# Softmax denominators by accumulating transfers in a fused cross-attention kernel on Trainium2

## The reference

```python
xq  = (1 + scale_q)  * norm(x_q)  + bias_q      # scale and bias from silu(t_vec) @ Wss + bss
xkv = (1 + scale_kv) * norm(x_kv) + bias_kv
q = (xq @ Wq + bq)                              # 4096 x 16 x 32
k, v = split(xkv @ Wkv + bkv)                   # 3202 x 16 x 32 each
attn = softmax(q k^T / sqrt(32))                # per head, over 3202 keys
out = x_q + ((attn @ v) @ Wp + bp)
```

## Time and profile before

| | |
|---|---|
| median of 3 runs | 2140.96 us (2140.28 to 2142.82) |
| profiled execution | 2138.16 us |
| its span, first to last instruction | 2136.4 us |
| granted tensor clock | 0.999 of full speed |
| busy: PE, DVE, ACT, POOL | 2114.3, 1923.6, 1802.1, 17.3 us |
| transfers | 212.35 MB, 35.1% of the 16 engines' span on SP's queue |

### The profile page before, as it was taken

How to read it: one execution, slowest core, us unless ns; L and a number is a source line. 1 busy time by engine, 2 the same in 40 slices (tenths; PEclk the granted TensorE clock), 3 DMA queues, 4 the chain that set the end, 5 groups by cost and what they waited for, 6 DMA issues and landing times.

```text
span 2136.4 us, 56258 instructions
## 1 busy us (share of the span) xinstructions
PE 2114.3 (99%) x25036; PEld 604.5 (28%) x25036; DVE 1923.6 (90%) x1197; ACT 1802.1 (84%) x1923; POOL 17.3 (1%) x28
## 2 busy tenths in 40 slices
PE   7999999999999999999999999999999999999998
PEld 3444322222222222222222222222222222222222
DVE  2435799999999999999999999999999999999998
ACT  1212799999999999999999999999999999999995
POOL 0001000000000000000000000000000000000000
PEclk9999999999999999999999999999999999999999
DMA  9346534223422343223422342223432332232321
GB/s 314 115 161 235 148 86 97 77 80 92 118 75 77 95 102 86 67 80 92 121 71 82 89 122 71 78 79 89 110 83 71 101 95 78 70 84 78 97 55 52
DMA packets 202260, 212.35 MB, mean 99 GB/s; under 512 B 18838, under 2 KB 136222, under 8 KB 202012
## 3 DMA queue, kind: packets, MB, share of 16 engines
q1 hardware_dynamic: 199468, 208.16, 35.1%
q10 hardware_dynamic: 2544, 0.53, 0.1%
HBM read 170.38 MB, written 38.26 MB: 98 GB/s over the span
## 4 chain that ended last, share of the span: by engine, by line
PE 98%; DVE 1%; DMA 0%; issue 0%; ACT 0%; POOL 0%; SPq 0%; DVEq 0%
PE bank L1152 40%; PE bank L1164 37%; PE bank L1222 5%; PE bank L1184 5%; PE bank L1056 4%; PE bank L1067 4%; PE bank L1195 1%; PE bank L1280 1%; PE bank L1036 0%; DVE stats L1507 0%; PE bank L1207 0%; DMA arena<-in_L_xcond_Wss_kv_dram 0%; DVE arena L1525 0%; PE bank L1001 0%; PE bank L1097 0%
## 5 line engine op out<-in xcount | busy, mean ns | idle before, releaser
L1411 ACT ACTIVATE arena<-bank,shift 128x1024 f32<-128x1024 f32 x1600 | 1692.5, 1114 | 132.9 <-PE bank L1152 131.4
L1738 DVE TENSOR_TENSOR arena<-arena 128x2048 f32<-128x2048 f32 x736 | 1641.3, 2283 | 60.7 <-ACT arena L1411 59.0
L1152 PE MATMUL bank<-qs,ks 32*64 32x512 f32 x12800 | 918.2, 613 | 1.2 <-ACT arena L1369 0.7
L1164 PE MATMUL bank<-arena,vg 128*32 128x512 f32 x6400 | 852.3, 605 | 1.2 <-ACT arena L1411 1.2
L1164 PEld LDWEIGHTS bank<-arena,vg 128*32 128x32 f32 x6400 | 125.9, 108 | 650.5 <-ACT arena L1411 650.5
L1152 PEld LDWEIGHTS bank<-qs,ks 32*64 32x64 f32 x12800 | 205.0, 129 | 366.4 <-ACT arena L1411 227.0
L1222 PE MATMUL bank<-wp,arena 128*32 128x168 f32 (+2 forms) x2464 | 153.6, 321 | 0.0
L1184 PE MATMUL bank<-xt,wq 128*32 128x256 f32 (+2 forms) x2016 | 143.0, 355 | 0.0
L1222 PEld LDWEIGHTS bank<-wp,arena 128*32 128x32 f32 x2464 | 80.1, 110 | 184.3 <-issue 165.4
L1369 ACT ACTIVATE arena<-bank,bk_c 128x512 f32<-128x512 f32 (+1 forms) x28 | 17.9, 642 | 128.6 <-PE bank L1056 120.5
L1184 PEld LDWEIGHTS bank<-xt,wq 128*32 128x32 f32 x2016 | 65.5, 110 | 150.8 <-issue 132.8
(11 more groups left out here) (97 smaller groups left out, 384.9 us busy)
## 6 DMA issues: line engine op xcount, KB each, us to landing
ks<-k_full SPq DMA_DIRECT2D x160, 320.0 KB, 3.1
vg<-v_full SPq DMA_DIRECT2D x160, 320.0 KB, 3.8
p_b<-p_tails SPq DMA_DIRECT2D x128, 128.0 KB, 4.2
arena<-in_x_dram SPq DMA_DIRECT2D x15, 1024.0 KB, 9.8
q_full<-qs SPq DMA_DIRECT2D x32, 256.0 KB, 2.0
out_dram<-arena SPq DMA_DIRECT2D x32, 256.0 KB, 2.5
x_normal<-arena SPq DMA_DIRECT2D x7, 1024.0 KB, 7.6
xin<-x_normal SPq DMA_DIRECT2D x28, 256.0 KB, 10.1
```

Source lines behind the costliest of these rows:

```text
L1152: mm = nc.tensor.matmul(bank[out, 2 * (i % RING) + h % 2, :], ks[rows_of(h), keys], qs[rows_of(h), g, :], start=True, stop=True)
L1164: mm = nc.tensor.matmul(bank[rows_of(h), o_bank(u), :], vg[:, t, rows_of(h)], pt[t % PR][:, h, :], start=(t == 0), stop=False, skip_group_ ...
L1411: nc.scalar.activation(pt[t % PR][:, 2 * pair:2 * pair + 2, :], bank[:, first:first + 2, :], ACT.Exp, scale=SCALE, bias=shift[:, g:g + 1]) ...
L1738: nc.vector.tensor_tensor(a[:, :, :], (pt[t - 1] if k <= 2 else a)[:, :, :], pt[t % PR][:, :, :], ALU.add).then_inc(p_added, 1)
```

## The change

The tensor engine no longer forms the sums over keys, except for the last unit. Instead:
- `first_folds` (SP) copies partitions 0 to 31 of `acc` and `odd`, for each of the four heads, into a tile `folds` of 2 x 512 per partition, 32 partitions a head.
- `fold` (POOL) adds partitions 32 to 63, 64 to 95 and 96 to 127 onto it with three rounds of four accumulating transfers, and a fourth round adds the tail keys' weights. Each round waits for the one before, head by head.
- VectorE joins the two halves and finishes the sum over 32 partitions with its 32 x 32 transpose and a reduction, inverts, spreads the reciprocal by a second transpose, and multiplies (`sum_folds`, `invert`, `spread`, `divide` in steps 11 to 14 of the next unit), for each unit rather than for each block. `l_sums` and `l_recip` in DRAM are no longer used for this.
- The 24th add is made for the last unit alone.
- The residual is made in DRAM for blocks 0 to 6: SP copies 512 rows of x to the output (`copy_x`), POOL adds the bias (`add_bias`) and each row tile (`add_output`) with accumulating transfers. Block 7 keeps the former way.
- Query projections are cut in three parts (176, 168, 168) in all units. Output and query projections now start right after one another: steps 1 to 12 and 13 to 23 for g > 0, with two pieces in step 23; for g = 0, 1 to 12, tail scores in 13, output projection in 16 to 23 as before.
- `on` has two buffers, by the block's parity; the last buffers `l_blk`, `l_t`, `l_a`, `l_c`, `r_blk`, `r_few` go.

The diff, cut to its core:

```diff
             def q_parts(m):
-                return 3 if m == NG - 1 else 2
+                return 3
...
             def added(u):
-                return ADDS * u
+                return (ADDS - 1) * u
+            FOLDS = P // DH
...
+                    def first_folds(u):
+                        sp.wait_ge(p_added, added(u + 1))
+                        if u == 0:
+                            sp.wait_ge(xs_out[4], 16)
+                        else:
+                            sp.wait_ge(l_step, 5 * (u - 1) + 2)
+                        for h in range(HG):
+                            sp.dma_start(folds[rows_of(h), :, :], both[u % 2][0:DH, :, h, :]).then_inc(fold_in, 16)
...
+                    def copy_x(b):
+                        sp.dma_start(out2[b * QB:(b + 1) * QB, :], x2[b * QB:(b + 1) * QB, :]).then_inc(x_copied[b % 2], 16)
...
                             if u > 0:
                                 load_kv(u, NC - 1)
+                                first_folds(u - 1)
                             if more:
                                 load_kv(u + 1, 0)
-                            if g == 1 and b > 0:
-                                store_y(b - 1, 0)
-                            if u > 0:
-                                store_l(u - 1)
...
-                                store_r(b - 1, NH)
-                                load_r(b - 1, NH)
                                 store_q(b, 3)
...
-                            if g > 0 and b > 0:
-                                store_y(b - 1, g)
...
+                    def add_bias(b):
+                        pool.wait_ge(x_copied[b % 2], 16 * (b // 2 + 1))
+                        pool.dma_start(out2[b * QB:(b + 1) * QB, :],
+                                       bp.rearrange("(a n) -> a n", a=1).broadcast_to([QB, H]),
+                                       accum_op=ALU.add).then_inc(b_added[b % 2], 16)
+                    def add_output(b, j):
+                        if j == 0:
+                            pool.wait_ge(b_added[b % 2], 16 * (b // 2 + 1))
+                        pool.wait_ge(job_taken, JOB[y_last(b, j)] + 1)
+                        pool.dma_start(out2[b * QB + j * P:b * QB + (j + 1) * P, :], y_sb[:, j, :],
+                                       accum_op=ALU.add).then_inc(y_out[j], 16)
+                    def fold(u):
+                        b, g = divmod(u, NG)
+                        for s in range(1, FOLDS + 1):
+                            for h in range(HG):
+                                if s == 1:
+                                    pool.wait_ge(fold_in, 16 * HG * (u + 1))
+                                else:
+                                    pool.wait_ge(folded[h], 16 * (FOLDS * u + s - 1))
+                                if s < FOLDS:
+                                    pool.dma_start(folds[rows_of(h), :, :], both[u % 2][s * DH:(s + 1) * DH, :, h, :],
+                                                   accum_op=ALU.add).then_inc(folded[h], 16)
+                                else:
+                                    if h == 0:
+                                        pool.wait_ge(pt_out, 16 * NG * (b + 1))
+                                    row = (g * HG + h) * TAIL
+                                    pool.dma_start(folds[h * DH:h * DH + 1, :, :],
+                                                   pt_dram[row:row + TAIL, b * QB:(b + 1) * QB].unsqueeze(0),
+                                                   accum_op=ALU.add).then_inc(folded[h], 16)
+                    for u in range(1, UNITS):
+                        b, g = divmod(u, NG)
+                        fold(u - 1)
+                        if b > 0 and g == 0:
+                            add_bias(b - 1)
+                        if b > 0:
+                            add_output(b - 1, g)
...
                     def first_side(u, b, t):
-                        if b > 0:
-                            if 1 <= t < 5:
-                                project_queries(u, b, 3, 0, t - 1)
-                            if 5 <= t < 7:
-                                denominators(u, u - 1, t - 5)
...
+                        if b > 0 and 1 <= t < 13:
+                            project_queries(u, b, 3, (t - 1) // FT, (t - 1) % FT)
+                        if t == 13:
                             tail_scores(u, b)
+                        if b > 0 and 16 <= t < 24:
+                            output(u, b - 1, 0, (t - 16) // NG, (t - 16) % NG)
                     def later_side(u, b, g, t):
...
+                        if b > 0 and 1 <= t < 13:
+                            output(u, b - 1, g, (t - 1) // NG, (t - 1) % NG)
+                        if b + 1 < NB and 13 <= t < 24:
+                            project_queries(u, b + 1, g - 1, (t - 13) // FT, (t - 13) % FT)
+                        if b + 1 < NB and t == 23:
+                            project_queries(u, b + 1, g - 1, 2, FT - 1)
...
+                    def sum_folds(v):
+                        for h in range(HG):
+                            dve.wait_ge(folded[h], 16 * FOLDS * (v + 1))
+                        nc.vector.tensor_tensor(folds[:, 0, :], folds[:, 0, :], folds[:, 1, :], ALU.add).then_inc(l_step, 1)
+                        dve.wait_ge(l_step, 5 * v + 1)
+                        nc.vector.transpose(blocks(l_sb[:, :]), blocks(folds[:, 0, :])).then_inc(l_step, 1)
+                    def invert(v):
+                        some = slice(v * QB // DH, (v + 1) * QB // DH)
+                        dve.wait_ge(l_step, 5 * v + 2)
+                        nc.vector.tensor_reduce(l_keep[:, some], blocks(l_sb[:, :]), op=ALU.add, axis=AX_X).then_inc(l_step, 1)
+                        dve.wait_ge(l_step, 5 * v + 3)
+                        nc.vector.reciprocal(r_keep[:, some], l_keep[:, some]).then_inc(l_step, 1)
+                    def spread(v):
+                        some = slice(v * QB // DH, (v + 1) * QB // DH)
+                        dve.wait_ge(l_step, 5 * v + 4)
+                        nc.vector.transpose(blocks(r_sb[:, :]), r_keep[:, some].unsqueeze(2).broadcast_to([P, QB // DH, DH])
+                                            ).then_inc(l_step, 1)
+                    def divide(v):
+                        b, g = divmod(v, NG)
+                        dve.wait_ge(l_step, 5 * v + 5)
+                        dve.wait_ge(tail_added, TAIL * (v + 1))
...
+                        nc.vector.tensor_tensor(on[b % 2][:, g, :], o_all[:, g, :], r_sb[:, :], ALU.mult).then_inc(on_ready, 1)
...
+                    def vector_side(u, t):
+                        b, g = divmod(u, NG)
+                        if u > 0:
+                            if t == 11:
+                                sum_folds(u - 1)
+                            if t == 12:
+                                invert(u - 1)
+                            if t == 13:
+                                spread(u - 1)
+                            if t == 14:
+                                divide(u - 1)
+                        if g == 0 and b + 1 < NB and t == 18:
                             turn_queries(b + 1)
...
                             if k == 1 and u >= 2:
-                                dve.wait_ge(job_done, DONE["l", u - 2] + 1)
...
+                                for h in range(HG):
+                                    dve.wait_ge(folded[h], 16 * FOLDS * (u - 1))
```

More of the change, by code:

```diff
@@ L220, in attention @@
             y_out = [sem(f"y_out{j}") for j in range(TPB)]
+            last_out = [sem(f"last_out{j}") for j in range(TPB)]
             turned = sem("turned")
@@ L1188, in project_queries @@
                             mm.then_inc(job_done, 1)
-                    def denominators(u, of, half):
-                        if half == 0:
-                            free(("l", of))
-                            pe.wait_ge(p_added, added(of + 1))
-                        for h in range(HG):
-                            mm = nc.tensor.matmul(bank[rows_of(h), side_bank(u), halves_of(half)], ones[:, :],
-                                                  acc[of % 2][:, h, halves_of(half)], start=True, stop=True,
-                                                  skip_group_check=True)
-                        if half == 1:
-                            mm.then_inc(job_done, 1)
                     def tail_scores(u, b):
@@ L1676, in add_bias, with range_so_far @@
+                    def range_so_far():
+                        some = slice(0, (UNITS - 1) * QB // DH)
+                        nc.vector.reduce_max(l_tops[:, 0, 0:1], l_keep[:, some], AX_X).then_inc(last_step, 1)
+                        nc.vector.reduce_max(l_tops[:, 1, 0:1], r_keep[:, some], AX_X).then_inc(last_step, 1)
+                    def add_bias():
+                        dve.wait_ge(xy_in, 16)
                         dve.wait_ge(bp_in, 16)
-                        rows = xy[b % 2]
@@ L1678, in add_bias @@
```

(8 more changed lines are left out.)

276 lines of the change are left out of this document (76 added, 200 removed).

## The result

| | before | changed |
|---|---|---|
| median of 9 runs | 2140.92 us | 2147.93 us |
| lowest to highest | 2139.08 to 2142.82 | 2143.92 to 2157.91 |
| profiled execution, its span | 2138.16, 2136.4 | 2157.91, 2156.1 |

The ratio is 1.0037, 95% interval 1.0023 to 1.0052: slower, by 7 us on the medians, where 20 us less had been forecast. The nine runs of the changed kernel lie 14.0 us apart, those of the kernel before 3.7. Its profiled execution is the slowest of the nine, 10 us above the median, so that the trace shows the trouble larger than the median has it.

A forecast was written before the change was run, and what follows sets the result against it. PE's steps were taken as the bound, other engines covered. Gains 13.4 + 2.4 + 2.7 + 1.8 = 20.3 us gave 2120.7 on the median, stated as 2120.5; forecast's own range 2113 to 2127, whole range 2112 to 2190.

The forecast's parts named there:

- 13.4 + 2.4 + 2.7 + 1.8: PE's gains in us: units g = 1 to 3 of blocks 1 to 6; g = 0 of blocks 1 to 7; units 1 to 3; 29 to 31.
- the short units: Units 1 to 3 and 29 to 31, forecast to gain 0.9 and 0.6 us each on PE.
- The end after the last exp is the same chain: After the kernel's last exp, the closing work was taken as unchanged, with no gain or cost.
- The double piece: PE's step 23 with two query pieces, g = 1 to 3: second piece costs 0.29 to 0.40, step taken as 2.69 us.
- the first rival: Late rounds stall DVE at step 11; each unit pays 4 x (round - 5.8), for 30 units; chance 0.22.
- the ring: Exp of step t + 5 waits for the add of step t, bounding VectorE's lag at 7 us.
- the allowance for the rounds: Copy plus four rounds before DVE's step 11: 25.3 us, 3 more before stalling; 5.1 or 5.8 us a round.
- the lag of 4.1: VectorE's lag in us after the six denominator operations, from 0.4 by step 10; the limit was 7.
- Sum about 24: Copy's issues and landing, 5 us, plus four rounds at 4.7, the last less: about 24 us, in time by little.
- VectorE starve POOL: Rival: POOL hands over transfers only between DVE's adds, 16 issues taking 35 us; about 2480 us; chance 0.05.
- DVE did not become the bound in the short units: Rival: DVE becomes the bound there, covered by only 0.6 us, or its lag stalls g = 0; 2125 to 2134; chance 0.08.
- PE did not wait for the takes: Rival: bare steps 14, 15 and the two-piece step delay the takes, PE waits for PSUM; 2138 to 2142; chance 0.03.

The follow-up runs named there:

- e1: The changed kernel with VectorE's four denominator steps starting in step 14 (13 where g = 0) instead of 11: 2118.92 us, ratio 0.9901 to the kernel before.
- e8: The changed kernel with VectorE's four denominator steps starting in step 12 instead of 11: 2119.74 us, ratio 0.9911 to the kernel before.
- e2: The changed kernel with VectorE's four denominator steps starting in step 9 instead of 11: 2297.49 us.
- e3: The changed kernel with all transfers made, but VectorE sums the bias tile instead of the folded sums and doesn't wait for them: 2119.15 us, ratio 0.9902.
- e5: The changed kernel without copy of x or bias, row tiles stored without accumulation, for blocks 0 to 6: 2149.21 us, ratio 1.0047.

## Why the prediction was wrong

**What held.** The order of work on PE gains what it was to gain: e1, the change with a delay of three steps (two where g = 0), is 20.2 us faster than before on the same chip, against the 20.3 of "13.4 + 2.4 + 2.7 + 1.8". That it agrees to 0.1 us is luck; the interval of the ratio allows 17.5 to 24.6 us. The main loop gained more: from step 1 to step 1 a unit with g > 0 went from 59.30 to 58.45 us and one with g = 0 from 60.16 to 59.54, 0.85 and 0.62 in place of 0.74 and 0.34, which makes about 24 with the short units (0.88 and 0.6, as worked out). And "The end after the last exp is the same chain" was wrong: it took 24.6 us before and 27.6 in e1, 3.0 more (29.3 in the changed kernel). Of the 3.0, 0.9 us in e8 is VectorE's final add starting later; the cause of the other 2.1, behind VectorE's last operation, is open. The double piece made a step of 2.61 (2.69 taken, between 2.62 and 2.73 by its bounds). VectorE's added work was 3.70 by the sum and is 0.69 + 0.71 + 0.68 + 0.25 + 0.70 + 0.68 = 3.71 in the trace. The place of the loss was named as well: the first rival, "the place is DVE's wait at step 11, behind it the adds, then the ring, then PE". It had a chance of 0.22. But the signs set for it did not tell. The rounds stayed "below 5.8 us each", the sign of being right, and the wait of 3.6 us lies between the two signs, "below 3 us" and "6 us or more".

**The step that failed** is the allowance for the rounds: "That leaves 25.3 us, and 3 more until the lag of 4.1 becomes 7", and from it "a round may take 5.1 us unseen and 5.8 without stalling the ring". The 3 us were taken as if each unit began with VectorE on time. But lag that VectorE is allowed to have is lag with which it makes its last add, and so starts the next transfers. A delay can be spent once, not in every unit. In steady state the allowance is PE's unit less VectorE's work from sum to copy: by the measured units 58.45 - 32.08 = 26.4 for g > 0 and 59.54 - 34.27 = 25.3 for g = 0, 26.1 over a block, where I had 28.3. In blocks 0 and 7 PE's unit with g > 0 is only 56.3 to 56.5 us long, and the allowance 24.2 to 24.4. e2 shows the closed loop by its slope (4.4 us a unit for two adds), e8 by its floor.

**A second term was mis-sized:** the chain, "Sum about 24", measured 27.0. The copy went as thought, 4.9 us on average from its first issue to POOL's first (4.6 to 6.3). The first three rounds nearly did, 4.85 us each from first issue to next first issue, where 4.7 had been taken. The end did not: from the last round's first issue to the sum it is 7.5 us, where less than 4.7 had been taken. A round counted from first issue to first issue follows head 0 alone; the last of the four heads is issued later, and its third round landed 4.4 us after head 0 had begun the fourth, into the loads of keys and values. The fourth of that head comes after it. With the mean of 27.0 the open window of 28.3 would still have covered; with 24 the closed one of 26.1 would have. Both errors together gave the wrong sign. The price in the rival, "4 x (round - 5.8), for 30 units", had the right form and the wrong threshold. With the closed allowance it is 30 x (27.0 - 26.1) = 27 us. Between the first and the last sum e3, where PE is the floor, takes 1751.2 us and the changed kernel's profiled execution 1786.9, 35.7 more. Most of the difference is that four of the 30 turns are the short ones of blocks 0 and 7, and a fifth is short in part. How long the chain was in the median run, 10 us quicker than the profiled one, no trace shows.

**The other rivals.** VectorE did not starve POOL: beside adds that run without a gap, an issue by itself took 0.83 us and four in a row 3.5, and e3 is as quick as it should be. What the Trainium skill (SBUF — State Buffer, Who interferes with whom) says of `tensor_tensor`, that it was not seen to stall transfers issued by GpSimd, agrees with that. The fit of the Trainium skill (DMA: Bandwidth & Descriptors, Anatomy of one DMA), by which a round was an estimated 3.2 us, does not: the changed kernel's first three rounds in the unit shown take (1140.04 - 1126.98) / 3 = 4.4 each, 4.85 on average over all units, and the measurement decides. DVE did not become the bound in the short units (e1 has all of the gain), and PE did not wait for the takes (its units are 58.45 and 59.54 us long in e3).

**The chances.** What is most worth noting is that the margin was called thin in the text, and 0.62 was put on it all the same. The direction came from a comparison of 24 with 28.3, both made of estimates for an operation that no row showed.

## What to carry to other kernels

When a result of one iteration is waited for in the next, write the loop down: the sum of all that lies on the closed path, one turn, against the period of the bound engine, in its shortest turns too. Slack in a ring or a buffer helps once; it does not add to the budget of each turn. And before a chain of small dependent transfers is given up, try where its result is first waited for: here one step later (e8) was the difference between 0.4% slower and 0.9% faster.

## What the runs showed of the hardware

- An accumulating transfer of 128 KB within SBUF, from POOL in rounds of four, landed 5.0 us after its issue in the median; a plain copy of the same shape from SP took 2.4 in the median. Accumulating 256 KB to DRAM took 4.3, 1 MB from a repeated row of bias 15.2.
- POOL took 0.83 us to issue one of 32 partitions and two rows each when it stood by itself, and 3.51 for four in a row; the mean of 1127 ns in the group's row is of issues that overlap. SP took 0.33 to 0.46 for loads that are larger, and 2.5 to 3.5 for its four copies in a row.
- The last round moves 4 KB a transfer and still landed after 3.1 us in the median.
- From the first copy to the sum the chain took 24.7 to 29.3 us from unit to unit, while VectorE's own part of the turn was constant to 0.01. Whether that is why the changed kernel's runs lie 14.0 us apart is not shown: e5, which waits for the chain as well, has four runs within 3.7 us, and e8, which hardly waits, four within 5.8.
